# Integer weights of an attention layer converted on another engine, with the step programs of three engines in another order

## The reference

```python
h = einsum('bct,bcd->bdt', x, cond_weights[condition])      # per-sequence 64x64 mixing
w = (qw - 8) * repeat(scales, 128, axis=0)                  # 4-bit integers, a scale per 128 rows
q, k, v = h @ w_q, h @ w_k, h @ w_v                         # 32 query heads, 8 key/value heads of 128
attn = softmax(where(causal, rope(q) @ rope(k).T / sqrt(128), min))
x = x + (attn @ v) @ w_o                                    # w_o quantized in the same way
x = x + ffn(cond2(x))                                       # session MLP with gelu, dense layer, LoRA experts
```

## Time and profile before

| | |
|---|---|
| median of 3 runs | 1975.27 us (1974.65 to 1975.47) |
| the profiled execution | 1964.11 us, its span 1962.0 us |
| busy in the span | TensorE 88%, VectorE 83%, ScalarE 70%, GpSimd 3% |
| mean granted TensorE clock | 0.971 of full |
| DMA | 87.68 MB, a mean of 45 GB/s |

### The profile page before, as it was taken

The page is one execution under the profiler, slowest core; times in us unless marked ns, Lnnn a source line. Parts: engine busy times, 40 slices in busy tenths (PEclk is TensorE's granted clock), DMA queues, the critical chain, the costliest instruction groups (busy, mean ns, idle before and its releaser), DMA issues.

```text
span 1962.0 us, 38762 instructions
## 1 busy us (share of the span) xinstructions
PE 1733.4 (88%) x14306; PEld 948.8 (48%) x14306; DVE 1629.2 (83%) x2692; ACT 1376.6 (70%) x2339; POOL 55.5 (3%) x50
## 2 busy tenths in 40 slices
PE   4688989998998999899989988998999767779999
PEld 3434544544454445455545444454545455554444
DVE  6598999988998999889989998999999868993222
ACT  2568888887888898778888887988888436960000
POOL 0200000000000000000000000000000001320000
PEclk8799999999999999999999999999999989999999
DMA  6321011020102010201011020102020121110111
GB/s 207 98 69 41 24 54 45 2 74 5 45 1 77 3 44 2 77 3 45 23 55 31 16 60 19 45 1 77 1 64 15 44 106 62 40 45 33 50 48 43
DMA packets 118064, 87.68 MB, mean 45 GB/s; under 512 B 13404, under 2 KB 108004, under 8 KB 117860
## 3 DMA queue, kind: packets, MB, share of 16 engines
q1 hardware_dynamic: 117220, 84.83, 14.3%
q10 hardware_dynamic: 640, 0.13, 0.0%
HBM read 76.55 MB, written 8.39 MB: 43 GB/s over the span
## 4 chain that ended last, share of the span: by engine, by line
PE 44%; DVE 28%; issue 10%; DMA 10%; ACT 5%; SPq 3%; DVEq 0%; POOL 0%; ACTq 0%
PE pj L1428 6%; PE pj L1430 5%; PE cx L1750 4%; DVE y L795 3%; PE tp L1440 3%; PE sa L1495 3%; DMA work<-sv_d 3%; DMA wts<-qo_d 3%; PE sbk L1495 3%; PE sa L1497 3%; PE sbk L1497 3%; DVE work L714 2%; DVE work L716 2%; PE ex L1750 2%; PE sa L1750 2%
## 5 line engine op out<-in xcount | busy, mean ns | idle before, releaser
L1152 ACT ACTIVATE pj<-pj,ratio 128x512 f32<-128x512 f32 x741 | 490.3, 676 | 99.8 <-PE pj L1430 95.9
L1428 PE MATMUL pj<-hid,wts 128*128 128x512 f16 x1024 | 394.9, 386 | 21.8 <-ACT pj L1152 14.0
L1430 PE MATMUL pj<-hid,wts 128*128 128x512 f16 x1024 | 392.8, 384 | 0.0
L1161 ACT ACTIVATE sbk<-sbk,wts 128x512 f32<-128x512 f32 x384 | 256.5, 668 | 38.7 <-PE sbk L1497 36.6
L1161 ACT ACTIVATE sa<-sa,wts 128x512 f32<-128x512 f32 x353 | 237.7, 673 | 62.0 <-PE sa L1497 60.4
L1440 PEld LDWEIGHTS tp<-wts,hid 128*128 128x128 f16 x3072 | 180.1, 98 | 35.8 <-issue 10.3
L1440 PE MATMUL tp<-wts,hid 128*128 128x128 f16 x3072 | 192.4, 219 | 0.0
L1428 PEld LDWEIGHTS pj<-hid,wts 128*128 128x128 f16 x1024 | 100.2, 98 | 174.8 <-ACT pj L1152 64.7
L1152 ACT ACTIVATE ex<-ex,ratio 128x512 f32<-128x512 f32 x224 | 152.8, 682 | 16.2 <-PE ex L1430 15.9
L1428 PE MATMUL ex<-hid,wts 128*128 128x512 f16 x256 | 99.1, 387 | 43.6 <-ACT ex L1152 31.3
L1430 PEld LDWEIGHTS pj<-hid,wts 128*128 128x128 f16 x1024 | 101.1, 99 | 72.5 <-issue 3.0
(11 more groups left out here) (242 smaller groups left out, 3288.0 us busy)
## 6 DMA issues: line engine op xcount, KB each, us to landing
wts<-qo_d SPq DMA_DIRECT2D x64, 256.0 KB, 3.2
y<-x_d SPq DMA_DIRECT2D x7, 2048.0 KB, 7.9
wts<-qq_d SPq DMA_DIRECT2D x35, 256.0 KB, 3.1
int_even<-qq_d SPq DMA_DIRECT2D x29, 256.0 KB, 2.9
out_d<-y SPq DMA_DIRECT2D x12, 512.0 KB, 2.6
work<-qv_d SPq DMA_DIRECT2D x16, 256.0 KB, 6.9
work<-sv_d SPq DMA_DIRECT2D x16, 256.0 KB, 9.0
work<-wb_d SPq DMA_DIRECT2D x8, 512.0 KB, 4.5
```

The lines of the kernel that those rows point to most:

```text
L1152: act.activation(unit_bank[u][:, :], unit_bank[u][:, :], ACT.Copy, scale=ratio[:, KT * u + j:KT * u + j + 1]).then_inc(u_scaled[u], 1)
L1161: act.activation(out_bank[t % 2][:, :], out_bank[t % 2][:, :], ACT.Copy, scale=o_ratio[:, REP * t + h:REP * t + h + 1]).then_inc(o_scaled[ ...
L1428: mm(bank[:, :], w_int[:, u, j, :], hid[:, 0, j, CH * c:CH * (c + 1)], start=j == 0, stop=False, skip_group_check=True)
L1430: mm(bank[:, :], w_int[:, u, j, :], hid[:, 1, j, CH * c:CH * (c + 1)], start=False, stop=True, skip_group_check=True).then_inc(u_done[u], 1)
```

## The change

`int_piece` and `wo_piece` become VectorE instructions (`tensor_scalar`, adding -8, SBUF to SBUF), at the places `pieces(0)` to `pieces(4)` of VectorE's step; the number of pieces a chunk stays. VectorE keeps two rescalings a step, (2, 2) and (3, 0) of the units; before it had five of the units, (1, 0), (1, 1), (1, 3), (4, 3), (4, 4), and `rescale_out(out4, 3, 0)`. ScalarE does the rest. `prob_high(p4, 1)`, the f16 copy of the second half's probabilities, goes to ScalarE. Of the f16 copies `rope_high`, ScalarE's is that of unit 3 where it was unit 2, in the steps and ahead of the first one. The step programs of VectorE, ScalarE and TensorE are put into another order. In VectorE's, `rope_cos(p4, 4)` stands ahead of `v_split`, and `soft_norm(p4, 0)` and `soft_mask(p4, 1)` ahead of `add_out(out4, 1)`, behind which `dequant_scale` is called. The pieces stand behind `rope_split(p4, 4)`, `rope_high(ahead, 0)`, `add_out(out4, 5)`, `rope_add(ahead, 2)` and `rope_split(ahead, 3)`. The DMAs and SyncE's program are the same.

```diff
--- before.py
+++ after.py
@@ -813,6 +813,20 @@
                 dve.tensor_scalar(out_bank[t % 2][:, :], out_bank[t % 2][:, :], o_ratio[:, REP * t + h:REP * t + h + 1], None,
                                   ALU.mult).then_inc(o_scaled[t % 2], 1)
 
+            def int_piece(g, p):
+
+                u, half = p // 2, p % 2
+                dve.wait_ge(int_in[p % 2], 16 * NU * g + 16 * (p // 2 + 1 - NU))
+                dve.wait_ge(u_done[u], KT * NC * g + (4 * half + 4 - KT))
+                dve.tensor_scalar(w_int[:, u, 4 * half:4 * half + 4, :].rearrange("p k n -> p (k n)"), int_stage[p % 2], -8.0, None,
+                                  ALU.add).then_inc(S["int_ready"], 1)
+
+            def wo_piece(g, t):
+
+                dve.wait_ge(wo_in[t % 2], 16 * CT * g + 16 * (t // 2 + 1))
+                need(dve, o_done[t % 2], upto((g, -1), CT * REP, REP * (t // 2) + REP))
+                dve.tensor_scalar(w_out[:, :, P * t:P * (t + 1)], wo_stage[t % 2], -8.0, None, ALU.add).then_inc(S["wo_ready"], 1)
+
...
-            def step(p4, ahead, out4, between):
-
+            def step(p4, ahead, out4, between, pieces):
+
+                rope_cos(p4, 4)
                 v_split(p4)
-                rope_cos(p4, 4)
                 rope_sin(p4, 4)
                 between("rope", 4)
                 soft_mask(p4, 0)
                 rope_add(p4, 4)
                 soft_max(p4, 0)
                 rope_high(p4, 4)
-                if ahead:
-                    rescale(ahead, 1, 0)
                 soft_shift(p4, 0)
                 rope_split(p4, 4)
+                pieces(4)
                 if out4:
                     add_out(out4, 0)
                     between("out", 0)
-                if ahead:
-                    rescale(ahead, 1, 1)
+                soft_norm(p4, 0)
+                soft_mask(p4, 1)
+                if ahead:
+                    rescale(ahead, 2, 2)
+                soft_max(p4, 1)
                 if out4:
                     add_out(out4, 1)
                     between("out", 1)
-                soft_mask(p4, 1)
-                soft_norm(p4, 0)
-                soft_max(p4, 1)
-                if out4:
-                    rescale_out(out4, 3, 0)
-                if ahead:
-                    rescale(ahead, 1, 3)
+                soft_shift(p4, 1)
+                if ahead:
                     rope_cos(ahead, 0)
                 prob_high(p4, 0)
+                prob_split(p4, 0)
                 if ahead:
                     rope_sin(ahead, 0)
                     between("rope", 0)
-                soft_shift(p4, 1)
                 if out4:
                     add_out(out4, 2)
                     between("out", 2)
-                prob_split(p4, 0)
+                soft_norm(p4, 1)
+                pt_copy(p4, 0)
+                if ahead:
+                    rescale(ahead, 3, 0)
+                    rope_add(ahead, 0)
+                    rope_cos(ahead, 1)
                 if out4:
                     add_out(out4, 3)
                     between("out", 3)
                 if ahead:
-                    rope_add(ahead, 0)
-                soft_norm(p4, 1)
-                pt_copy(p4, 0)
-                if ahead:
-                    rope_cos(ahead, 1)
                     rope_high(ahead, 0)
+                pieces(0)
+                if ahead:
                     rope_sin(ahead, 1)
                     between("rope", 1)
-                prob_high(p4, 1)
+                prob_split(p4, 1)
                 if ahead:
                     rope_split(ahead, 0)
                     rope_add(ahead, 1)
-                prob_split(p4, 1)
+                    rope_cos(ahead, 2)
+                    rope_high(ahead, 1)
+                pt_copy(p4, 1)
                 if out4:
                     add_out(out4, 4)
                     between("out", 4)
                     add_out(out4, 5)
                     between("out", 5)
-                if ahead:
-                    rope_high(ahead, 1)
-                pt_copy(p4, 1)
+                pieces(1)
                 if ahead:
                     rope_split(ahead, 1)
-                    rope_cos(ahead, 2)
                 ctx_lo(p4, 0)
                 if ahead:
-                    rescale(ahead, 4, 3)
                     rope_sin(ahead, 2)
                     between("rope", 2)
+                    rope_add(ahead, 2)
+                pieces(2)
+                if ahead:
                     rope_cos(ahead, 3)
-                    rescale(ahead, 4, 4)
-                    rope_add(ahead, 2)
-                ctx_lo(p4, 1)
-                if ahead:
+                    rope_high(ahead, 2)
+                    rope_split(ahead, 2)
                     rope_sin(ahead, 3)
                     between("rope", 3)
-                    rope_split(ahead, 2)
                     rope_add(ahead, 3)
                 if out4:
+                    add_out(out4, 6)
+                    between("out", 6)
+                ctx_lo(p4, 1)
+                if out4:
                     add_out(out4, 7)
-                    between("out", 6)
-                if ahead:
-                    rope_high(ahead, 3)
-                if out4:
-                    add_out(out4, 6)
                     between("out", 7)
                 if ahead:
                     rope_split(ahead, 3)
+                pieces(3)
                 between("end", 0)
 
             def group(g, first=False, last=False):
+                def int_pieces(i):
+                    if i < NU - 1:
+                        int_piece(g + 1, 2 * i)
+                        int_piece(g + 1, 2 * i + 1)
+
...
+                    pieces = (wo_pieces, no_pieces, no_pieces if last else int_pieces, no_pieces if last else last_int_pieces)[c]
                     ahead = (g, c + 1) if c + 1 < NC else (None if last else (g + 1, 0))
-                    step((g, c), ahead, None if first and c == 0 else (g, c - 1), between)
+                    step((g, c), ahead, None if first and c == 0 else (g, c - 1), between, pieces)
 
             score_factors()
...
                 rope_add((0, 0), u)
-                if u in (0, 1, 3):
+                if u in (0, 1, 2):
                     rope_high((0, 0), u)
                 rope_split((0, 0), u)
...
-            def step(p4, ahead, out4, more, pieces):
+            def prob_high(p4, h):
+                act.wait_ge(S["probs"], upto(p4, 2, h + 1))
+                need(act, S["tp_done"], upto(p4, 2, h))
+                act.activation(pp[:, 0, :], sm[:, h, :, :].rearrange("p b s -> p (b s)"), ACT.Copy).then_inc(S["probs_hi"], 1)
+
+            def step(p4, ahead, out4, more):
 
                 v_hi(p4)
                 if ahead:
+                    rescale(ahead, 0, 0)
+                if out4:
+                    rescale_out(out4, 0, 0)
+                if ahead:
                     rescale(ahead, 2, 0)
-                    rescale(ahead, 0, 0)
+                    rescale(ahead, 0, 1)
                 if out4:
                     rescale_out(out4, 1, 0)
-                    rescale_out(out4, 0, 0)
-                if ahead:
-                    rescale(ahead, 0, 1)
+                    rescale_out(out4, 0, 1)
+                if ahead:
+                    rescale(ahead, 0, 2)
+                if out4:
+                    rescale_out(out4, 1, 1)
+                if ahead:
+                    rescale(ahead, 1, 0)
+                if out4:
+                    rescale_out(out4, 0, 2)
+                if ahead:
+                    rescale(ahead, 0, 3)
+                exps(p4, 0)
+                if ahead:
                     rescale(ahead, 2, 1)
-                if out4:
-                    rescale_out(out4, 0, 1)
-                if ahead:
-                    rescale(ahead, 0, 2)
-                if out4:
-                    rescale_out(out4, 1, 1)
-                if ahead:
-                    rescale(ahead, 2, 2)
-                if out4:
-                    rescale_out(out4, 0, 2)
-                if ahead:
-                    rescale(ahead, 0, 3)
+                    rescale(ahead, 0, 4)
+                    rescale(ahead, 1, 1)
                 if out4:
                     rescale_out(out4, 1, 2)
                 if ahead:
-                    rescale(ahead, 2, 3)
-                    rescale(ahead, 0, 4)
-                exps(p4, 0)
-                pieces(4)
-                if ahead:
                     rescale(ahead, 0, 5)
...
+                if ahead:
+                    rescale(ahead, 1, 3)
+                if out4:
+                    rescale_out(out4, 3, 0)
+                    rescale_out(out4, 2, 2)
                 if ahead:
                     rescale(ahead, 1, 4)
...
                     rescale(ahead, 3, 1)
-                if out4:
-                    rescale_out(out4, 4, 0)
+                    rescale(ahead, 2, 5)
+                prob_high(p4, 1)
+                if ahead:
```

(83 more changed lines are left out.)

138 lines of the change are left out of this document (72 added, 66 removed).

## The result

The changed kernel takes 1918.97 us in the median of 4 runs (1917.04 to 1921.15), the kernel before 1974.96 beside it (1968.48 to 1975.47): ratio 0.9724, 95% interval 0.9701 to 0.9748, some 54 us less. The forecast was 1934, range 1905 to 1980: the time lies inside, 15 us under the likeliest. The profiled execution took 1917.04 us, its span 1915.0. The kernel before spreads more than the changed one: over all runs of this document from 1957.48 us (granted clock 0.973) to 1977.91 (0.963). Its profiled execution, 1964.11 us, is one of the shorter, so the two traces show a gain of 47 us where the ratio gives 54.

A forecast was written before the change was run, and what follows sets the result against it. No engine alone bounds the kernel; the queues wait for one another. Stalls of 61.8 us removed, 21 given back, gain about 41: profiled 1964.11 becomes 1923, as a median 1934 us; range 1905 to 1980.

The forecast's parts named there:

- The two stalls of 61.8 us go: TensorE's waits in the 32-step stage: 31.2 us for VectorE's `rescale_out(out4, 3, 0)`, 30.6 us for ScalarE's `ex` rescalings, both removed.
- ScalarE's fuller queue gives 21 us back: ScalarE, fuller by 3.3 and 2.0 us in chunks 1 and 3, returns half, 2.7 us a group, as waits.
- The clock explains little: In four windows, one per chunk, the clock was granted at 0.97 or 1.00, so it hardly explains step differences.
- The 433 us behind the last `v_split` stay: The time after the steps, 433 us, and the prologue stay as they are.
- A conversion costs 0.42 us: Each int32 to f16 piece on VectorE costs 0.42 us, like the f32 to f16 cast; bounds 0.42 to 0.75.
- Sums of VectorE by chunk: VectorE's work in chunks 0 to 3: 42.1, 37.6, 42.5, 41.4 us; about 50 us less over the run.
- Chunk lengths: Steps after the change: chunk 0 43 to 45 us, chunk 1 42 to 43.5, chunk 2 43 to 45, chunk 3 45 to 48.
- Waits for transfers: DMA waits of the conversions: none on ScalarE, under 10 us on VectorE, hidden behind the instructions between pairs.
- `rope_cos` ahead of `v_split` for nothing: VectorE's swap makes scores up to 0.75 us later, costed at nothing; 23 us if not hidden.
- VectorE as the bound: Rival, 0.14: conversions at 0.69 to 0.75 us fill chunks 0 and 2, taking back 32 to 40 us; 1966 to 1975.
- The exponentials: Rival, 0.17 with other new waits: `exps(p4, 0)`, now 13th in ScalarE's step, blocks its queue; about 2005 at 1.5 us each.
- the stalls only move: Rival, 0.06: order does not matter, TensorE's stalls move to other banks; 1971 to 1979.

## Why the prediction was right, point by point

*The two stalls of 61.8 us go.* Right, and each is worth about its size: 36 us alone for the rescaling (row 31.2), 35 alone for the conversions off ScalarE (row 30.6). Their sum, 71, is 17 more than the change brought; in the traces 29.4 and 31.2 us of steps, 60.6, against 40.3. That value and row agree is in part chance: waits elsewhere grew, and 4.5 and 10.7 us of it are TensorE's busy time, which the prediction did not count.

*ScalarE's fuller queue gives 21 us back.* Wrong in the mechanism; this is the step that failed, "half of it, 2.7 us a group or 21 us", a choice without a row behind it. ScalarE's sum came as worked out over four windows (38.1 + 40.1 + 37.6 + 40.0 = 155.8 forecast, 156.1 measured), though not window by window (39.7, 37.9, 39.5, 39.0), but TensorE waits for it 6.6 us in all. What came back came from VectorE: `rescale(3, 0)` and rope, 43 us of waits at places that the prediction did not look at, though the rows of the change (rescalings kept, ahead of them softmax) name one. That moving the one took back 27 us shows it. The size was near by luck: in the steps 21.5 us of the 61.8 came back (61.8 - 40.3), against 21, but as the difference of two things that the sum had not: some 33 us of other waits came in, and 11.6 us of TensorE's own busy time went.

*The clock explains little.* Not so: those 11.6 us, over a quarter of what the steps gained. A mean of 0.97 in the window of chunk 3 is not the upper level throughout: 3.4 us in it ran at 0.50, behind the stall at `sa`.

*The 433 us behind the last `v_split` stay.* Nearly: 426.3 after 432.8, and 4.6 of the difference are the last wait for L813.

*A conversion costs 0.42 us.* Right: 0.418, the cast's 0.416. The Trainium skill, "VectorE: DVE Perf Modes", section "The perf-mode tier table", which gave no int32, is borne out as it was read: int32 went as fp32 does, and with two sources it took 0.684.

*Sums of VectorE by chunk.* 42.1, 37.6, 42.5 and 41.4 forecast; 41.8, 38.3, 42.2 and 41.7 measured. Over the run -43.5 us instead of -50: instructions overlap (the rescaling at 708.25 lasts 0.75 and the next begins after 0.66), so one removed frees less than its length, and one added costs less: the conversions alone raised VectorE's busy time by 43.3 us (1629.2 to 1672.5), not 56.

*Chunk lengths.* Chunk 3 (45.9, forecast 45 to 48) and 2 (45.0, 43 to 45) as forecast, chunk 1 just under (41.9, 42 to 43.5); chunk 0 at 45.9 outside 43 to 45, because the loop turn moved into it. The same move flatters chunk 3: with the 2.7 us of the turn counted as before, the two are 43.2 and 48.6, so chunk 0 hits and chunk 3 just misses.

*Waits for transfers.* Right: none on ScalarE, 1.5 us on VectorE, no conversion with any idle time ahead of it. *`rope_cos` ahead of `v_split` for nothing.* Right, by the run that turns it back.

*The rivals.* VectorE as the bound has the right mechanism (36.5 us of it brought 38 us of time) and failed by the price alone. The exponentials wait 1.0 us in three pieces: refuted. That the stalls only move: refuted for the whole change by its time. Where an order alone was changed, most of the stall did move: from `sa` to `pj` with the rescaling earlier (0.7% gained), and from rope to ScalarE with the quanta swapped (nothing gained).

What stays open: whether the two single moves add up on the kernel before, which was not tried; what the new orders add to the moves; and why 7 of the 18 waits of 1.9 us and more in the steps before had no fall of the clock beside them.

## What to carry to other kernels

Where in-order queues of nearly equal load feed one another, cost an instruction by who waits for it and what stands ahead of it in its queue, not by its engine's sum: 0.75 us a step was worth a gain of 36 us, a gain of 27, or a loss of 8 or 14. Look at the granted clock behind each stall too: here it made 11.6 of 40.3 us. After a move, list anew each instruction left on the fuller engine that frees a bank of TensorE, and look what its program puts ahead of it; a lump "half comes back" hides the next fix. Measure the halves of an exchange between two full engines together, since each alone can lose.

## What the runs showed of the hardware

A conversion of 128x512 from int32 to f16 took GpSimd 1.49 to 1.66 us (means of its groups in two runs; spans on GpSimd are rough), 3.6 to 4 times VectorE's 0.418, and still helped, since GpSimd is idle. It slowed some of VectorE's instructions with two SBUF sources beside it: the same line (min/median/max ns), with the conversions on GpSimd and on VectorE:

```profile
L785 DVE TENSOR_TENSOR work<-work x160: 675/685/1094, 96.4 to 1452.8; 128x512 f32<-128x512 f32 x160
```

```profile
L761 DVE TENSOR_TENSOR work<-work x160: 680/684/694, 96.5 to 1467.1; 128x512 f32<-128x512 f32 x160
```

The median is the same, the longest 0.4 us more: a few were held up, not all slowed. Of the 160, 17 ran beside a GpSimd conversion; the 7 that took over 0.725 us are all among them. Of the 256 additions to `y` (L819), which read PSUM, 63 ran beside one, and none of the 256 took over 0.753 us. The Trainium skill, "SBUF — State Buffer", section "Who interferes with whom", says that an instruction of VectorE with two SBUF inputs contends with GpSimd's reads for one shared port; these rows agree, though the price is small: in the steps a mean of 704 ns instead of 686 on this line, 3 us over 156 instructions, and of 719 instead of 687 on L789, 4 us over 125.
